# Linear attention and experts: moving max and exp of one token group ahead of the variance of the next

## What is computed

```python
xn = _layernorm(x, axis=-1)                        # x: 4 x 4096 x 1024, f32
# in _L0_attn_ref
K = elu(x @ Wk + bk) + 1;  V = x @ Wv + bv;  Q = elu(x @ Wq + bq) + 1
KV   = einsum('nshd,nshm->nhmd', K, V)             # 16 heads of 64
Ksum = K.sum(axis=1)
Z = 1 / (einsum('nlhd,nhd->nlh', Q, Ksum) + 1e-6)
out = einsum('nlhd,nhmd,nlh->nlhm', Q, KV, Z) @ Wo + bo
x = layer_norm(x + out);  y = relu(x @ W1 + b1) @ W2 + b2;  return layer_norm(x + y)
# in _L0_ffn_ref: for each of 8 experts, acc += w_e * (relu(xn @ W1e + b1e) @ W2e + b2e)
x = x + _L0_attn_ref(xn, ...) + _L0_ffn_ref(xn, ...)
```

## Time and profile before

| | us |
|---|---|
| median of 3 runs | 5873.01 |
| profiled execution, device time | 5869.37 |
| its span on the slowest core (core 3) | 5867.7 |
| the other cores' spans | 5855.0 to 5867.8 |
| mean granted TensorE clock, core 3 | 0.912 |

### The profile page before, as it was taken

One profiled execution on the slowest core, in us unless ns is written; L12 is line 12 of the kernel. 1 busy time (PEld: TensorE's weight loads), 2 busy tenths in 40 slices (PEclk: granted clock), 3 DMA queues, 4 the chain that ended last, 5 costly groups with the idle time before them and its releaser, 6 DMA issues.

```text
span 5867.7 us, 55904 instructions; the slowest of 8 cores (5855.0 to 5867.8 us)
## 1 busy us (share of the span) xinstructions
PE 4836.1 (82%) x21665; PEld 2125.3 (36%) x21665; DVE 1784.5 (30%) x3367; ACT 1045.2 (18%) x2045; POOL 344.5 (6%) x661
## 2 busy tenths in 40 slices
PE   4677499999999999999999999999975434777722
PEld 2333144444444444444444444444432211333301
DVE  3444222222222222222222222222224254111173
ACT  3444111111111111111111111111102100111100
POOL 1000000000000000000000000000000000000000
PEclk8888799999999999999999999999987666999965
DMA  3000122222222222222222222222212110111103
GB/s 59 32 30 26 19 38 40 35 38 38 36 37 40 35 38 38 36 37 40 36 37 38 37 36 40 38 35 38 38 24 40 45 22 11 27 26 27 26 0 115
DMA packets 105683, 209.47 MB, mean 36 GB/s; under 512 B 12960, under 2 KB 13232, under 8 KB 105424
## 3 DMA queue, kind: packets, MB, share of 16 engines
q0 software_dynamic: 91056, 163.84, 17.9%
q1 hardware_dynamic: 14368, 42.06, 2.2%
HBM read 361.06 MB, written 8.39 MB: 63 GB/s over the span
## 4 chain that ended last, share of the span: by engine, by line
PE 77%; DVE 11%; ACT 5%; DMA 4%; issue 3%; POOL 0%; DVEq 0%; ACTq 0%; SPq 0%; POOLq 0%
PE ps L709 31%; PE ps L747 30%; PE ps L1067 4%; PE ps L1046 4%; PE ps L471 2%; ACT h_b L1056 1%; DMA xt_b<-xs 1%; DMA xtm_b<-xs 1%; PE ps L753 1%; DVE x_sb L1084 1%; PE ps L451 1%; DVE ln_t L1012 1%; DVE ln_t L1014 1%; PE ps L930 1%; DVE vtm L522 1%
## 5 line engine op out<-in xcount | busy, mean ns | idle before, releaser
L709 PE MATMUL ps<-xnbf,w1s 128*128 128x512 bf16 x8192 | 1826.5, 381 | 53.7 <-DVE wb L694 32.4
L709 PEld LDWEIGHTS ps<-xnbf,w1s 128*128 128x128 bf16 x8192 | 799.6, 98 | 1047.1 <-issue 106.7
L747 PE MATMUL ps<-h_hi,w2s 128*128 128x512 bf16 x4096 | 923.5, 384 | 22.5 <-DVE acc L771 22.5
L747 PE MATMUL ps<-h_lo,w2s 128*128 128x512 bf16 x4096 | 904.9, 379 | 0.0
L771 DVE TENSOR_TENSOR acc<-acc,ps 128x512 f32<-128x512 f32 x992 | 615.3, 683 | 835.4 <-PE ps L747 533.1
L747 PEld LDWEIGHTS ps<-h_hi,w2s 128*128 128x128 bf16 x4096 | 404.9, 99 | 521.6 <-issue 51.3
L719 ACT ACTIVATE h_lo<-ps,eb_sb 128x512 bf16<-128x512 f32 x512 | 310.1, 688 | 1541.2 <-PE ps L709 1541.2
L747 PEld LDWEIGHTS ps<-h_lo,w2s 128*128 128x128 bf16 x4096 | 400.9, 98 | 483.2
L719 ACT ACTIVATE h_hi<-ps,eb_sb 128x512 bf16<-128x512 f32 x512 | 310.2, 688 | 1462.9 <-PE ps L709 1462.9
L727 DVE TENSOR_TENSOR h_lo<-h_lo,wb 128x512 bf16<-128x512 bf16 x512 | 183.4, 420 | 948.0 <-ACT h_lo L719 948.0
L727 DVE TENSOR_TENSOR h_hi<-h_hi,wb 128x512 bf16<-128x512 bf16 x512 | 183.3, 420 | 899.9 <-ACT h_hi L719 899.9
(11 more groups left out here) (178 smaller groups left out, 2250.3 us busy)
## 6 DMA issues: line engine op xcount, KB each, us to landing
w1s<-ew_pk POOLq DMA_DIRECT2D x256, 256.0 KB, 3.5
w2s<-ew_pk POOLq DMA_DIRECT2D x256, 256.0 KB, 3.5
xtm_a<-xs SPq DMA_DIRECT2D x32, 512.0 KB, 3.5
xt_b<-xs SPq DMA_DIRECT2D x32, 256.0 KB, 2.5
w1s<-w_pk POOLq DMA_DIRECT2D x32, 256.0 KB, 3.5
w2s<-w_pk POOLq DMA_DIRECT2D x32, 256.0 KB, 3.5
xtm_b<-xs SPq DMA_DIRECT2D x16, 512.0 KB, 4.0
out<-otm_b SPq DMA_DIRECT2D x16, 512.0 KB, 2.9
```

What stands on the lines that cost most here:

```text
L709: self.em("T", lambda t, k=k, tt=tt, slot=slot: t.matmul(ps[tt][:], self.w1t(slot, k), self.xnbf[:, k * TOWN + tt * 512:k * TOWN + (tt + 1 ...
L747: self.em("T", lambda t, j=j, tt=tt, slot=slot, hreg=hreg, lp=last_plain: t.matmul(ps[4 + tt][:], self.w2t(slot, j), hreg[:, j * TOWN + tt ...
```

## The change

`emit_stats` gets two hooks. `mid_v` is called after the subtraction L409 is written and before the variance reduction on VectorE; `mid_s` after the scaling L414 is written and before Ln on ScalarE. `emit_elu` is split in three: `elu_vmax` (the max, with its waits), `elu_sexp` (the exp, with its waits) and `elu_vtail` (min-add and V copy, with theirs). In turn g `elu_vmax(g-1)` is called at the first hook, `elu_sexp(g-1)` and `elu_vtail(g-1)` at the second. The operations and their waits are the same as before.

The order of a turn on VectorE becomes L400, L402 (g), max (g-1), variance reduction and its scaling (g), min-add and V copy (g-1), sums (g-1). On ScalarE: square and subtraction (g), exp (g-1), Ln up to the multiplication and the copies (g), PSUM copies (g). TensorE's and SyncE's order stays. The first turn has no group before it, and the last group's max, exp, min-add and V copy come after the loop in the old order.

```diff
-        def emit_stats(g):
+        def emit_stats(g, mid_v=None, mid_s=None):
...
             self.em("S", lambda s, xt=xt, mc=mc: s.add(xt, xt, mc))
             s_sub = self.inc("S", self.s_sc, 1)
+            if mid_v is not None:
+                mid_v()
             self.wait("V", self.s_sc, s_sub)
             self.em("V", lambda v, sq=sq, ac=ac: v.reduce_sum(ac, sq, axis=AXX))
             self.vbar()
             self.em("V", lambda v, ac=ac: v.tensor_scalar(ac, ac, INV_D, EPS_LN, op0=OP.mult, op1=OP.add))
             v_ac = self.inc("V", self.s_ve, 1)
+            if mid_s is not None:
+                mid_s()
             r0 = self.scol[:, 3:4]
             self.wait("S", self.s_ve, v_ac)
...
-        def emit_elu(g, evKmm, evVmm):
+        def elu_vmax(g, evKmm):
...
             evK_v[g] = self.inc("V", self.s_ve, 1)
+
+        def elu_sexp(g, evKmm):
...
             self.wait("S", self.s_mm, evKmm)
             self.wait("S", self.s_ve, evK_v[g])
...
             evK_s[g] = self.inc("S", self.s_sc, 1)
+
+        def elu_vtail(g, evVmm):
...
             self.wait("V", self.s_sc, evK_s[g])
...
         for g in range(NGL):
-            emit_stats(g)
-            if g >= 1:
+            if pend:
                 pg, ek, ev = pend.pop(0)
-                emit_elu(pg, ek, ev)
-                emit_kv(g - 1)
+                emit_stats(g, mid_v=lambda pg=pg, ek=ek: elu_vmax(pg, ek),
+                           mid_s=lambda pg=pg, ek=ek, ev=ev: (elu_sexp(pg, ek),
+                                                             elu_vtail(pg, ev)))
+                emit_kv(pg)
+            else:
+                emit_stats(g)
             ek, ev = emit_T(g)
             pend.append((g, ek, ev))
         pg, ek, ev = pend.pop(0)
-        emit_elu(pg, ek, ev)
+        elu_vmax(pg, ek)
+        elu_sexp(pg, ek)
+        elu_vtail(pg, ev)
         emit_kv(NGL - 1)
```

More of the change, by code:

```diff
@@ L492, in emit_T @@
             return evKmm, evVmm
-        def emit_elu(g, evKmm, evVmm):
+        def elu_vmax(g, evKmm):
             par = g % 2
-            kslot = self.ktm[:, par * D:(par + 1) * D]
-            vslot = self.vtm[:, par * D:(par + 1) * D]
             rt = self.elu_a[:, par * D:(par + 1) * D]
@@ L505, in emit_elu @@
             evK_v[g] = self.inc("V", self.s_ve, 1)
+        def elu_sexp(g, evKmm):
+            par = g % 2
+            kslot = self.ktm[:, par * D:(par + 1) * D]
             self.wait("S", self.s_mm, evKmm)
@@ L513, in emit_elu @@
             evK_s[g] = self.inc("S", self.s_sc, 1)
+        def elu_vtail(g, evVmm):
+            par = g % 2
+            kslot = self.ktm[:, par * D:(par + 1) * D]
+            vslot = self.vtm[:, par * D:(par + 1) * D]
+            rt = self.elu_a[:, par * D:(par + 1) * D]
             self.wait("V", self.s_sc, evK_s[g])
```

## The result

| | before | after |
|---|---|---|
| executions compared, lowest to highest, us | 5864.9 to 5877.4 | 5883.6 to 5893.5 |
| ratio after / before, 95% interval | | 1.0026 (1.0016 to 1.0036) |
| loop of phase A, core 3 | 537.55 | 556.05 |
| span, core 3 | 5867.7 | 5879.0 |

The changed kernel is 0.26% slower, some 15 us (9 to 21): clear of noise, and within the 2% that count as no change.

The account below looks back on a forecast made before the run. The prediction took a chain of waits to bound the token loop, with no engine full. Later transposes (+5 us) and two lost full-clock K blocks (+5) made +10 on 5873, so 5883 us, range 5866 to 5900.

Parts of the forecast that it names:

- What bounds the loop: Phase A's token loop: no engine full; a chain of waits from e, the end of K's bias matmuls, sets its pace.
- VectorE: Variance reduction waits behind the previous group's max; the K and V chain moves by 0 to 0.13 us a turn.
- held-up min-add: VectorE's min-add (L516) could be delayed by the variance reduction and its scaling, by 0 to 0.13 us; taken as 0.
- ScalarE: Ln waits behind exp, so the statistics release the transposes 7.45 us (own tokens) or 6.89 us (others) after K's bias.
- The sum over 31 turns: Later or earlier transposes in the edited turns, each at its former clock, add up to +4.6, say +5 us.
- The clock: TensorE's K blocks: two of eight full-clock blocks lost at 2.4 us each, +5 us; bounds +19 and -19.
- 540 to 555: Sign of being right: phase A's loop takes this many us instead of 537.55.
- rival 2: Every K block at half clock: +24 us, 5897 us; chance 0.22 with the cases between (+15 to +30).
- rivals 1 and 2: First: statistics release the transposes, +5 to +15 us, chance 0.55; second: all K blocks at half clock, +24, chance 0.22.
- The rule of the Trainium skill: Matmul bursts after a long wait start throttled; taken strictly, every K block at half clock, sum +24 rather than +10.
- Rival 3: Exp first pays: full-clock K blocks come in rows; eight more give -14 us, 5859 us; chance 0.20 (under +5).
- Rival 4: Later TensorE start tips V blocks to half clock: up to +136 us, 6009 us; chance 0.02 with other slow surprises.

Follow-up runs that it names:

- e5: Changed kernel with the five small ScalarE operations that refine the statistics' scale replaced by one copy; loop 518.07 us, ratio to before 0.9964.
- e10: Changed kernel plus unused matmuls: eight behind the V block, three between the transpose waves, four behind the second; loop 479.22 us, ratio to before 0.9911.
- e11: Kernel before the change plus unused matmuls: eight behind the V block, three between the transpose waves, four behind the second; loop 521.65 us, ratio 0.9987.
- e7: Kernel before the change with the five small ScalarE operations that refine the statistics' scale replaced by one copy; loop 520.63 us.
- e2: Only exp moved ahead of Ln against the kernel before, the max left behind the variance reduction; loop 538.04 us, ratio 1.0018 (0.9995 to 1.0041).
- e3: Changed kernel plus eight unused matmuls of 512 columns behind each V block; loop 514.05 us.
- e12: Exp ahead of Ln, max behind the variance reduction, plus unused matmuls behind V, between and behind the transpose waves; loop 467.86 us, ratio to before 0.9886.
- e9: Kernel before with KV matmuls behind the next K block, max ahead of KV additions, seven unused matmuls between and behind transposes; loop 430.38 us, ratio 0.9854.
- e6: Kernel before with the KV matmuls moved behind the next group's K block and their additions behind the following statistics; loop 454.46 us.

## Why the prediction was right, and where it was not

- *What bounds the loop.* Right: a chain of waits from e, with the V copy at e+4.27 before and after.
- *VectorE.* The variance reduction started at e+1.38 (said 1.4), L416 ended at 220.38 = e+2.85 (said 218.81-215.87 = 2.94). The held-up min-add, bounded at 0 to 0.13 us, came out at 0: e+2.80 against e+2.81.
- *ScalarE.* Ln at e+2.95 (said 3.04), transposes at e+7.43 (said 7.45), and for other tokens 435.52-428.65 = e+6.87 (said 6.89). The sum over 31 turns was +4.3 (said +4.6). e5 shows the step once more: a shorter chain takes it back. All of these are the terms of the chain of waits, and they came out to 0.1 us a turn.
- *The clock.* The mechanism was named, its size was off. I took two of eight full K blocks as lost, +5; all eight went. By the price of 2.4 us a block that would be +19, but the other blocks were shorter too (a mean of 6.08 us, against 6.34 for the 24 of before, and not the 6.54 of the turn I had read), so the K blocks cost +9.0. And I had priced only the K block: the transposes ahead of it also ran more often at the low clock, +5.1. Together +14 where the sum had +5. That is the term which was mis-sized, and why +18.5 stands where +10 was foretold for the loop; 556.05 us is also just outside the 540 to 555 named as a sign of being right (cores 0 to 2 are inside). In count the case was rival 2 (no full K block), in price between rivals 1 and 2, at the edge between the +5 to +15 and the +15 to +30 of the chances.
- *The total.* 5883 us was foretold, and the median of the executions compared is 5884.3. That close a hit is luck in part: the 5873 from which it was counted is 3 us above the median of the executions of before that were compared (5869.9), which hides the same amount of the loss.
- *The rule of the Trainium skill.* The Trainium skill ("TensorE: Matmul & The Clock Gate", section "HAM oscillation — how this bites in real kernels") has matmul bursts behind a long wait start throttled. In after 31 of 32 K blocks did, though after the loop's first wait none of TensorE's was longer than 2.1 us. The +24 that the prediction made of it was too much: the blocks were shorter than the one turn from which the 2.4 us came.
- *Rival 3*, that exp first pays once the clock is up, is wrong for this kernel as it stands and right as a mechanism: e10 against e11 is -42 us in the loop. The prediction's own rows for turns behind a full block (-1.54 for 15 and -1.04 for 16) make that -40, but it named nothing that would raise the clock in every turn.
- *Rival 4* did not come: V's matmuls have the same mean of 380 ns before and after.

What stays open: which property of the stretch ahead of the K block decides over its clock. Stretches from e to the transposes of 6.5 us gave 7 and 8 full blocks (e7, e5), 7.1 and 6.5 gave two (e2), 7.4 and 6.9 none, but length and order changed together in those runs. Length alone doesn't decide: in before, all eight full blocks stand behind stretches of 6.4 to 6.5 us, and so do 11 that are not full. With the fill, stretches summing to the same 223 us go with 0 (after), 10 (e3) or 31 full blocks (e10), so what TensorE does in the stretch counts. How much of it is needed was measured only for this fill in these places.

## What to carry to other kernels

Ask of a moved instruction not only what it releases but what was hidden under the work that it now stands behind: in most turns the statistics ended 5.2 us before the transposes needed them, and putting exp ahead of Ln made them the last wait of every turn (e2); the max ahead of the variance added 0.35 us to each. Price the halves apart: the moved max lost at either clock, and the moved exp won 54 us of the loop with the fill (e11 to e12), but nothing without it (e2, 538.04 against 537.55). Where TensorE's stretches end at either clock level, the same reordering can change sign with the clock (+18 us in the loop as it stands, -42 us with the clock held up), so look first at what keeps the clock down. Here unused matmuls in TensorE's waits took 77 us off the loop of the changed kernel (16 off that of before), and moving the KV matmuls behind the K block took 83 off that of before; the last of these removes the wait itself, with no work added.

## What the runs showed of the hardware

Unused matmuls were not waste: in e10 there are 473 more than in after (2393 instructions against 1920), and the loop is 77 us shorter (479.22 against 556.05). Where they stand matters: eight behind the V block lifted 10 of 32 K blocks of after to full clock, seven more between and behind the transposes lifted 31; in e9 those seven alone lifted 29 from 1. I had expected the fill behind V to do. On core 3 of every trace here each K block ended at full clock, however it had begun, and each V block behind it took at most 3.63 us, so the falls of the clock lie between the end of a V block and the inside of the next K block. A start at full clock is no promise either: of 20 such K blocks in e3 ten lost it inside, and of 7 in e6 all did.
